# A graph layer on one core: product, turn and the evacuation in another order in the first 25 rounds

## What is computed

```python
xn = layernorm(x)                                  # x: 3125 x 256
spmm = lambda h: segment_sum(edge_weight[:, None] * h[dst], src, 3125)   # 53125 edges
h = spmm(xn)                                       # a sparse adjacency times the rows
a0 = softmax(spmm(h) @ W0.T + b0)                  # layer 0
a1 = softmax(spmm(concat([a0, a0], 1)) @ W1.T + b1)
gnn = tanh(concat([a0, a1], 1) + h)
q, k, v = heads(xn @ wq.T), heads(xn @ wk.T), heads(xn @ wv.T)     # 4 heads of 64
k, v = layernorm(k) * gk + bk, layernorm(v) * gv + bv
mix = (q @ (k.T @ v / 3125)) @ wo.T + bo
x = x + gnn + mix
y = layernorm(x)                                   # gate: the best of 8 experts, capacity 489
x = x + expert(y) * probability                    # relu(y @ w1 + b1) @ w2 + b2, dropped beyond capacity
```

## Time and profile before

| | us |
|---|---|
| median of 3 runs | 1124.24 |
| lowest, highest | 1123.86, 1127.8 |
| the profiled execution, its own time | 1116.33 |
| its span | 1114.6 |
| TensorE busy in the span | 1061.4 |
| VectorE busy in the span | 715.7 |
| ScalarE busy in the span | 314.4 |
| GpSimd busy in the span | 199.2 |

### The profile page before, as it was taken

How to read it: one execution, slowest core, us unless ns; L and a number is a source line. 1 busy time by engine, 2 the same in 40 slices (tenths; PEclk the granted TensorE clock), 3 DMA queues, 4 the chain that set the end, 5 groups by cost and what they waited for, 6 DMA issues and landing times.

```text
span 1114.6 us, 15224 instructions
## 1 busy us (share of the span) xinstructions
PE 1061.4 (95%) x5377; PEld 663.0 (59%) x5377; DVE 715.7 (64%) x1608; ACT 314.4 (28%) x1042; POOL 199.2 (18%) x243
## 2 busy tenths in 40 slices
PE   5899999999999999999999999999999799999995
PEld 3466566666665665666784444644458466666664
DVE  8999999897776876869840111237777445444444
ACT  4777777312212122222211111111112211212220
POOL 2234454400101010110000000000434411111111
PEclk9999999999999999999999999999999799999998
DMA  6120011123333333423269988987993676555510
GB/s 177 19 58 21 28 49 48 49 95 134 132 133 132 133 132 133 180 96 142 96 226 352 380 291 323 337 323 280 321 321 139 171 216 148 133 133 139 145 39 7
DMA packets 80985, 178.57 MB, mean 160 GB/s; under 512 B 35678, under 2 KB 64122, under 8 KB 68750
## 3 DMA queue, kind: packets, MB, share of 16 engines
q1 hardware_dynamic: 67592, 123.39, 34.7%
q10 hardware_dynamic: 9190, 46.12, 10.4%
q0 software_dynamic: 4128, 8.08, 2.1%
HBM read 116.23 MB, written 63.77 MB: 161 GB/s over the span
## 4 chain that ended last, share of the span: by engine, by line
PE 79%; DVE 10%; issue 3%; ACT 3%; DMA 2%; POOL 1%; SPq 0%; POOLq 0%; ACTq 0%; DVEq 0%
PE ps L1669 23%; PE ps L1823 20%; PE ps L1925 9%; PE ps L1913 8%; PE ps L1653 7%; PE ps L1626 2%; PE ps L1692 2%; PE ps L1559 2%; PE ps L1612 2%; PE ps L1648 1%; ACT W L821 1%; DVE bst L1223 1%; DMA xbuf_dram<-XX,sidx 1%; DMA RING<-xbuf_dram 1%; POOL rbuf_dram L745 1%
## 5 line engine op out<-in xcount | busy, mean ns | idle before, releaser
L1669 PE MATMUL ps<-RING,XX 128*128 128x512 f32 (+2 forms) x700 | 296.2, 548 | 1.5 <-DVE W L1181 1.5
L1823 PE MATMUL ps<-RING,RY 128*128 128x512 f32 (+4 forms) x750 | 269.5, 516 | 0.1
L1823 PEld LDWEIGHTS ps<-RING,RY 128*128 128x128 f32 x750 | 134.3, 191 | 118.8 <-issue 111.3
L854 ACT COPY RING<-ps 128x512 f32<-128x512 f32 (+3 forms) x163 | 92.5, 568 | 278.9 <-PE ps L1653 259.6
L1669 PEld LDWEIGHTS ps<-RING,XX 128*128 128x128 f32 x700 | 117.5, 190 | 68.9 <-issue 61.6
L1174 DVE TENSOR_TENSOR RING<-RING,RY 128x1536 bf16<-128x1536 bf16 (+1 forms) x150 | 140.0, 940 | 4.0
L1653 PEld LDWEIGHTS ps<-RING 128*128 128x128 bf16 x1575 | 100.6, 97 | 52.0 <-issue 46.4
L1164 DVE TENSOR_TENSOR RING<-iota_p,RY 128x1024 bf16<-128x1024 bf16 (+1 forms) x150 | 96.8, 652 | 29.0 <-PE ps L1653 26.5
L1653 PE MATMUL ps<-RING 128*128 128x128 bf16 (+1 forms) x1575 | 113.0, 217 | 0.0
L985 ACT ACTIVATE RY<-ps,b1T 128x489 f32<-128x489 f32 x64 | 42.9, 670 | 171.2 <-PE ps L1913 171.2
L1526 DVE SCALAR_TENSOR_TENSOR W<-ps,RING,W 128x256 f32<-128x256 f32 (+1 forms) x32 | 15.5, 484 | 90.0 <-PE ps L1925 89.0
(11 more groups left out here) (279 smaller groups left out, 1329.7 us busy)
## 6 DMA issues: line engine op xcount, KB each, us to landing
RING<-adj_dram SPq DMA_DIRECT2D x60, 1280.0 KB, 7.2
adj_dram<-RING ACTq DMA_DIRECT2D x30, 1280.0 KB, 4.6
rbuf_dram<-W SPq DMA_DIRECT2D x8, 516.0 KB, 5.2
RING<-rbuf_dram SPq DMA_DIRECT2D x8, 516.0 KB, 4.0
xbuf_dram<-W SPq DMA_DIRECT2D x8, 512.0 KB, 3.2
XT<-in_L_ffn_w SPq DMA_DIRECT2D x16, 256.0 KB, 5.7
XT<-in_L_ffn_w SPq DMA_DIRECT2D x4, 1024.0 KB, 9.0
RING<-in_L_ffn_w SPq DMA_DIRECT2D x16, 256.0 KB, 4.9
```

What stands on the lines that cost most here:

```text
L854: nc.scalar.copy(RING[:, n % 2, at:at + w], ps[:, u % 2, 0:w]).then_inc(s_bev, 1)
L1669: last = nc.tensor.matmul(ps[:, ACC + dd, 0:w], XN[:, j, dd * H:(dd + 1) * H], at[:, i * w:(i + 1) * w], start=(j == 0), stop=True, skip_g ...
L1823: last = nc.tensor.matmul(o, (Y if l == 0 else S0)[:, j, :], RING[:, slot_of[g % 5], i * across + first:i * across + first + w], start=(j ...
```

## The change

TensorE and ScalarE write their rounds in another order. On TensorE, from round 2 on, product stands behind build, and turn of the next tile behind apply. On ScalarE the evacuation of a block, with its transfer, stands ahead of squares. No instruction is added or left out.

```diff
@@ ScalarE
                 if it < NT:
                     paired(it)
-                    squares(it)
-                if it == 2:
-                    roots(1)
                 if 0 <= u < NU:
                     evac(u)
                     if u - 1 in [strip_end(k) for k in range(NS)]:
                         strip_out(strip_of(u - 1))
+                if it < NT:
+                    squares(it)
+                if it == 2:
+                    roots(1)
                 if 1 <= it <= NT:
                     kept(it - 1)
@@ TensorE
             for it in range(NU + 4):
-                if it < NT:
+                if it < 2:
                     product(it)
                 if it < NT:
                     ranks(it)
...
                 if 0 <= it - BUILD_IT < NU:
                     build(it - BUILD_IT)
+                if 2 <= it < NT:
+                    product(it)
                 if 1 <= it <= NT:
                     slots(it - 1)
                 if KV_LAG <= it < NT + KV_LAG:
                     kvprod(it - KV_LAG)
-                if it + 1 < NT:
-                    turn(it + 1)
...
                 if 0 <= it - APPLY_IT < NU:
                     apply(it - APPLY_IT)
+                if it + 1 < NT:
+                    turn(it + 1)
```

## The result

| | before | after |
|---|---|---|
| median, us (4 runs each, side by side) | 1124.25 | 1157.9 |
| lowest, highest | 1123.86, 1127.8 | 1157.32, 1158.45 |
| profiled execution, its own time | 1116.33 | 1157.62 |
| its span | 1114.6 | 1155.6 |

The ratio is 1.031, with a 95% interval of 1.0289 to 1.0331: the change costs 33.65 us. The forecast was 1154, in a range of 1143 to 1166. Sign, range and the main mechanism held. Two terms of the sum were mis-sized, in opposite directions, one was missing, and one came out at its size by another way than was foreseen.

What follows compares the result with a forecast made beforehand. VectorE was taken to bound the kernel until about 68 us and around iteration 16, TensorE from 68 to 124 us. Terms 20.4 - 2.1 + 4.8 + 5 + 1 = 29.1, rounded to 30, gave 1154 us, range 1143 to 1166.

Steps and rivals of the forecast that it cites:

- Part 1: TensorE, rounds 7 to 15 and 17 to 24: with turn behind apply, build waits for weigh, 17 x 1.2 = 20.4 us.
- The holes of the earlier trace: TensorE's four longer rounds, where turn waited for a late kept: 0.51 us each should go, -2.1 us.
- a loop over GpSimd: Product behind build closes a loop through squares, kept, GpSimd's widening and the next build: 7.16 us or 9.31 us.
- Part 2: Rounds where GpSimd's work meets VectorE's long products after head_var: six such rounds at 0.8 us, 4.8 us.
- P: GpSimd's time from its start after kept to build's release: 3.83 us beside VectorE's long products, 1.68 beside a waiting VectorE.
- rival (a): GpSimd's loop binds in every round: 44.5 us more, 1169 us; chance 0.07.
- Part 3: First rounds: product of iteration 2 comes late, delaying squares and roots, and rounds 3 to 6 wait: 5 us.
- Rival (e): TensorE's granted clock falls to its lower level for all 17 rounds: 58 us more, above 1200 us; chance 0.01.
- Part 4: The way out at iteration 25: build waits longer for GpSimd as kept ends later, 1 us.
- the way to the end: After iteration 25 both orders are the same program, so the delay goes to the end in full.

## Why the prediction was right, and where it was not

**Right: Part 1, the wait for weigh.** It was sized at 0.99 to 1.37 us a round, 1.2 taken. Measured are, in the round at 100.59, 1.07 us of idle time (from the turn's end at 100.82 to build at 102.49, less ranks 0.60), 0.24 for the slower first matmuls of build, and 0.18 back from the shorter turn: 1.13, and a round of 8.05. Cutting the wait (weigh first) and the loop behind it brought the round to 6.73, so this is shown. The holes of the earlier trace rows went as said. Not foreseen was that this term is hidden behind another: with turn put back the time does not change, since product's move alone costs 1.0 us a round. The prediction had a loop over GpSimd, but not the wait of turn for kept that stands in its place when turn stays.

**Too high: Part 2, the contended rounds.** Six rounds at 0.8 us were taken, 4.8 in all. Seven rounds (10 to 12, 15, 20 to 22) came out 0.25 to 0.33 us above 8.06: 1.9 in all. The loop's arithmetic held: 5.48 us plus a GpSimd time of 110.67 - 107.86 = 2.81 gives 8.29, measured 8.32. The step that failed is the choice of P nearer to 3.83. Head_var holds VectorE back, as foreseen (3.54 us, below), but that shifts its long products behind GpSimd's sum, so that only the cast meets the first of them. VectorE in order of time, with its idle time in brackets:

```profile
107.65 0.18 DVE L1117 TENSOR_SCALAR hvar<-hvar 128x40 f32<-128x40 f32 x1 [3.54 <-ACT W L821]
108.42 1.78 DVE L1105 TENSOR_TENSOR RY<-iota_k,HB 128x2304 bf16<-128x2304 f16 x1
```

The sum (108.29, 0.69 us) ran while the compare had hardly begun; the cast (108.98, 1.69 us) ran beside it. How near the full size was, the late head_var and the old ScalarE order showed, with a P of 3.85 and 3.87 us. Rounds 16 and 20 of the latter, at the high clock, take 9.84 us; the rounds of 11 us have the low clock on top. The Trainium skill (GPSIMD Engine Reference, section 1, Specifications) says that GpSimd contends with VectorE instructions that have two SBUF inputs. These rows agree. Taken for every round it was rival (a), and that didn't come: in most rounds VectorE waited for GpSimd.

**Too low: Part 3, the first rounds.** 5 us were taken, 7.8 was the bound; 10.06 + 4.63 = 14.7 were measured. The chain around round 2:

```profile
34.46 2.44 PE ps L1560 x15
36.90 3.73 PE ps L1627 x4
40.65 0.59 ACT RING L818
...
43.03 0.28 DVE lna L1015
```

The copy of the product comes at 40.65 instead of 33.62, 7.0 us later and not 3: the fifteen small matmuls of others alone take 2.44, and product 3.73 at the low clock. VectorE then waits 4.89 us for the roots (43.03 instead of 38.16). The bound allowed it 1 us, though the same row would have given it: roots follow the copy in ScalarE's order, and VectorE had no slack there, with 9.52 of 10 us busy. Putting the product back for rounds 2 and 3 returned 6.5 us, and with the product at the head of every round apply of round 4 came at 51.14, so the 10.06 us hang on product's place; rounds 5 and 6 then took 19.05 us instead of 21.21 (16.58 before). What holds the rest of these two rounds stays open. Rival (e), the clock, came in these rounds (the extra matmuls returned 3.4 us in the trace) and after the stops of rounds 6 and 16, but not in the steady ones.

**Missing: rounds 6 and 16.** "Round 16 stays VectorE's in both" was wrong, and it is the same for round 6 inside part 3. TensorE's order of time in round 16:

```profile
161.56 0.36 PE L1601 MATMUL ps<-HB,before 128*128 128x468 bf16 x1 [3.25 <-DVE HB L1102]
...
162.34 1.92 PE L1649 MATMUL ps<-RING 128*128 128x128 f32 x8
164.04 2.54 PE L1627 MATMUL ps<-wkvT,XT 128*128 128x512 f32 x4
...
168.00 1.88 PE L1670 MATMUL ps<-RING,XX 128*128 128x512 f32 x4
```

VectorE's preparation is as long as before, 5.66 us to the end of the reduce (5.64 before). But product used to run while TensorE waited for VectorE's reduce; now it stands behind ranks, which wait for that reduce, and behind build. Before, TensorE waited 1.53 us there and took 4.7 us from the reduce's end (136.20) to apply (140.90). Now it waits 3.25, and from 161.42 to 168.00 are 6.58 us. 1.43 of the longer way is build and product at a lower clock (1.71 and 2.33 us in the chain, instead of 0.89 and 1.72). With the product at the head of the round the wait was 1.19 and the round 9.92 us, and round 6 took 10.07 instead of 12.53. With the waits of build cut it stayed at 12.00, and with head_var late at 12.17. So the cause is the product's place. Of the clock's part in round 16 no run here is a test of its own; the nearest are the rounds of 11.45 and 9.84 us with ScalarE's order put back, which lie 1.6 us apart behind equal waits.

**Right in size, not in its way: Part 4; right: the way to the end.** 1 us was taken, 1.28 came. But it was to come from build's wait for GpSimd in round 25, as kept ends later, and that wait is the same as before, 2.17 us (2.18 before). What is new stands behind it, in TensorE's order of time: kvprod (L1634) waits for VectorE's normed, which head_var's wait for squares (5.02 us in this round) has made late.

```profile
237.34 1.13 PE L1649 MATMUL ps<-RING 128*128 128x128 f32 x8 [2.17 <-POOL RING L707]
...
240.64 0.71 PE L1634 MATMUL ps<-W 128*128 128x129 f32 x4 [0.90 <-DVE W L1133]
```

So this size was luck. The delay went to the layers in full. By the parts, 3.5 us too much in the steady rounds, 9.7 too little in the first ones and 2.1 missing at round 16 make the 37.2 of the trace; the medians differ by 33.65. That the forecast came within 4 us of the median is thus in part luck: in errors that cancel and in a profiled execution of before that was quick in its layers. The stated bounds are also 2 to 3 us wider than their own terms: the wait at 0.99 without contended rounds gives 16.8 - 2.1 + 5 + 1 = 20.7 us, 1145, and all upper values give 23.3 - 2.1 + 7.3 + 7.8 + 2.4 = 38.7 us, 1163; the measured 1157.9 lies inside these too.

## What to carry to other kernels

Where each engine takes its instructions in order, look at what stands between a producer and the step that another engine waits for: a matmul put behind a step that waits for a late engine loses the cover that it had, and a step that feeds another engine should stand early enough that the other engine's work fits before its use. When one wait is removed, work out the next-longest loop through all engines before pricing the gain; here undoing the one of two moves brought nothing, and undoing the other half. The stages in which another engine sets the pace deserve the same order-of-time reading as the steady one: 16.8 of the 37.2 us lost lay in rounds 0 to 6 and in round 16.

## What the hardware showed that was not expected

The turn of a tile, two transposes, takes 0.22 us of TensorE's chain behind apply and 0.41 behind kvprod; the difference of 0.19 us is 3% of a round of 6.73 us.

A stop of TensorE of 1.07 us in each round of 8.06 us, and of 1.34 to 1.42 us in the four longer ones among them, left the granted clock at the higher of its two levels through all nine rounds from 84 to 156 us, as the first row of the changed kernel's stretches shows (columns as above). After the one stop of 3.25 us in round 16 the next 5 us were granted 0.66, in the second row:

```profile
84.00:156.00 72.00, 61.08 (x384) 38.46 (x383) 56.50 (x73) 49.58 (x229) 21.34 (x39) 1.00 0.09 37
...
161.50:166.50 5.00, 4.94 (x17) 3.29 (x18) 4.97 (x6) 0.62 (x2) 0.00 (x0) 0.66 0.01 3
```

The loss falls on the work behind the stop, where TensorE is busy throughout (4.94 of 5 us). The length of a stop alone does not tell whether the clock falls: with ScalarE's order put back it fell behind a wait of 2.86 us and not behind the next, of 2.88. The Trainium skill (TensorE: Matmul & The Clock Gate, "HAM oscillation") describes a loop that falls back to the lower level in every turn. The waits in that loop are much longer than the stops of the steady rounds here, so these rounds neither bear it out nor speak against it.

GpSimd's cast of 128x512 from bf16 to f32 took 0.62 us beside a waiting VectorE and 1.69 beside its long bf16 compare, its sum over v 0.69 and 1.82. In these rows the instruction that started first kept its usual time, and the one that started beside it took longer. In the changed kernel the sum (108.29) kept its 0.69 us; the compare that started into it (108.42) took 1.78, where it took 1.36 in round 16 with GpSimd idle; and the cast, started into the compare, took 1.69. With head_var late the compare started first (115.21) and kept its 1.36 us, and GpSimd's small addition (115.39) took 1.23 instead of 0.20. The starts lay only 0.13 and 0.18 us apart.
